# Cross attention with clipped scores: keys on the partitions, one exponential per unit, sums by a product with ones

## The reference, cut to what matters

```
q = state @ Wq            # [128 tokens, 1024], 16 heads of 64
k, v = ctx @ Wkv          # [128 keys, 1024] each
s = (q_h @ k_h.T) * 0.125 # per head, [queries, keys]
s = clip(s, -5, 5)        # and a key that is masked out gets -5
p = exp(s) / sum over keys of exp(s)
out = concat_h(p @ v_h) @ Wo + bo
state = layernorm(state + out)
```

## Time and profile before

| what | value |
|---|---|
| median of 3 runs | 1938.68 us (1937.98 to 1938.98) |
| the profiled execution: its span, first to last instruction | 1932.0 us |
| what lies around the span, median less span | 6.7 us |
| mean granted TensorE clock | 0.960 of full |
| PE, DVE, ACT, POOL busy | 90%, 71%, 69%, 43% |
| L2_xattn in the span | about 970 to 1224 us |

### The profile page before, as it was taken

The page is one execution under the profiler, slowest core; times in us unless marked ns, Lnnn a source line. Parts: engine busy times, 40 slices in busy tenths (PEclk is TensorE's granted clock), DMA queues, the critical chain, the costliest instruction groups (busy, mean ns, idle before and its releaser), DMA issues. The chain is left out here.

```text
span 1932.0 us, 40599 instructions
## 1 busy us (share of the span) xinstructions
PE 1736.0 (90%) x13884; PEld 1294.5 (67%) x13945; DVE 1378.8 (71%) x3901; ACT 1340.0 (69%) x5411; POOL 837.3 (43%) x998
## 2 busy tenths in 40 slices
PE   6999999999888898789999999615889999999998
PEld 6886558889655565246688888404556777777777
DVE  4667886777888898988844444595998656566665
ACT  3447986565899996159977777442988666666666
POOL 2235770000566785147733333121776433333345
PEclk9999999999988999789999999866999999999999
DMA  7000000000000000000000000200000000000000
GB/s 285 1 1 1 2 2 2 1 2 2 2 1 2 2 2 2 1 1 2 2 2 1 2 1 2 117 0 1 1 2 2 1 1 1 1 1 1 1 1 23
DMA packets 5819, 22.98 MB, mean 12 GB/s; under 512 B 624, under 2 KB 2672, under 8 KB 4720
## 3 DMA queue, kind: packets, MB, share of 16 engines
q1 hardware_dynamic: 5616, 20.39, 2.7%
HBM read 19.34 MB, written 1.05 MB: 11 GB/s over the span
## 5 line engine op out<-in xcount | busy, mean ns | idle before, releaser
L1394 POOL TENSOR_TENSOR a_probs<-a_probs,a_rinv 128x512 f32<-128x512 f32 x352 | 365.7, 1040 | 318.0 <-DVE a_rinv L1238 314.5
L1047 ACT ACTIVATE a_probs<-bank,a_negmax 128x128 f32<-128x128 f32 x896 | 324.8, 434 | 12.9 <-DVE a_negmax L1218 12.8
L1394 POOL TENSOR_TENSOR c_probs<-c_probs,c_rinv 128x512 f32<-128x512 f32 x192 | 200.1, 1042 | 163.5 <-DVE c_rinv L1238 160.4
L889 PEld LDWEIGHTS bank<-const,a_probs 128*128 128x128 f32 x1408 | 159.0, 144 | 134.0 <-issue 110.2
L1047 ACT ACTIVATION_READ_ACCUMULATOR a_probs<-bank,a_negmax 128x1 f32 x896 | 237.5, 275 | 0.0
L889 PE MATMUL bank<-const,a_probs 128*128 128x128 f32 x1408 | 231.4, 288 | 1.9 <-DVE a_probs_t L1245 0.9
L1422 POOL TENSOR_TENSOR a_rstd<-a_ve,neg_half 128x1 f32<-128x1 f32 x128 | 70.2, 549 | 341.1 <-DVE a_ve L1296 340.9
L1218 DVE TENSOR_REDUCE a_negmax<-bank 128x4 f32<-128x512 f32 x224 | 152.0, 680 | 20.5 <-PE bank L857 16.6
L857 PE MATMUL bank<-a_kz,a_qk 32*128 32x512 f32 x512 | 148.1, 655 | 2.2 <-DVE a_probs L1216 1.6
L1238 DVE RECIPROCAL a_rinv<-a_rsum 128x4 f32<-128x4 f32 x352 | 59.7, 170 | 113.7 <-ACT a_probs L1043 107.8
L1245 DVE COPY a_probs_t<-bank 128x512 f32<-128x512 f32 x176 | 120.5, 684 | 25.8 <-PE bank L889 24.7
(11 more groups left out here) (254 smaller groups left out, 4418.9 us busy)
## 6 DMA issues: line engine op xcount, KB each, us to landing
w_L_ffn<-in_L_ffn SPq DMA_DIRECT2D x1, 3184.0 KB, 20.4
w_L_xattn<-in_L_xattn SPq DMA_DIRECT2D x1, 2112.0 KB, 29.5
w_L_xattn<-in_L_xattn SPq DMA_DIRECT2D x1, 2050.0 KB, 9.9
w_L_attn<-in_L_attn SPq DMA_DIRECT2D x1, 1345.5 KB, 23.1
w_L_attn<-in_L_attn SPq DMA_DIRECT2D x1, 1157.0 KB, 6.7
ctx_t<-in_ctxT SPq DMA_DIRECT2D x1, 1024.0 KB, 13.0
w_L_attn<-in_L_attn SPq DMA_DIRECT2D x2, 512.0 KB, 14.7
ctx<-in_ctx SPq DMA_DIRECT2D x1, 1024.0 KB, 13.3
```

What stands on the lines that cost most here:

```text
L889: mm = pe.transpose(bank[:, j * S:(j + 1) * S], Pb[:, n % PB, j * S:(j + 1) * S], ident)
L1047: op = act.activation(p, bank_of("scores", n)[:, j * width:(j + 1) * width], ACT.Exp, bias=negmax[:, n % PB, j:j + 1], accum_out=rsum[:, n ...
L1394: pool.tensor_tensor(p, p, along(rinv[:, n % PB, 0:heads], 512 // heads), ALU.mult).then_inc(sems["norm_done"], 1)
```

## The change

The scores are formed with the keys on the output's partitions. The queries lie packed in `Qs` (scaled by 0.125 in one copy), both operands of a head take 64 rows of the array, and the products of the two halves alternate, into two banks; a pair of units is scored together. The clip's upper bound is then one number per partition. One exponential covers the whole unit, without sums. For a pair of units PE forms the sums over the keys by a product with a tile of ones, 64 columns wide, so that the sum stands on all 64 partitions of a head, and then the values, without a transpose before. DVE inverts the bank of sums, 128x512, and multiplies the bank of values by it on the way to `OT` (`divide`, emitted after `inverse` and ahead of the projections' copies in each slot). POOL no longer scales the probabilities. The slots of the stages, of the projections and of the output move. The zeroing block of the first loop is gone. The mask is loaded as 128x16 bytes, element by element.

```diff
-    "h64c": [("q0", 9, "act"), ("q1", 7, "act"), ("k0", 6, "dve"), ("k1", 5, "dve"), ("v0", 4, "act"), ("v1", 2, "act")],
+    "h64c": [("q0", 7, "act"), ("k0", 6, "dve"), ("q1", 5, "act"), ("k1", 4, "dve"), ("v0", 3, "act"), ("v1", 2, "act")],
...
+    "scores": {"all": 3, "h8": 6, "h8p": 6, "h8r": 6, "moe": 4, "h64c": 4, "h64m": 6, "ffn": 4},
+    "max": {"all": 3, "h8": 6, "h8p": 5, "h8r": 6, "h64c": 4, "h64m": 5, "ffn": 4},
+    "front": {"all": 3, "h8": 5, "h8p": 4, "h8r": 5, "lin": 2, "h64c": 3, "h64m": 4},
...
+    "second": {"all": 0, "h64c": 1},
...
+    "values": {"all": -1, "h8": -2, "h8p": -2, "h8r": -2, "h64c": 1},
+    "outs": {"all": -1, "h8": -2, "h8p": -2, "h8r": -2, "h64c": 1, "lin": -2, "ffn": -2},
...
+    "output": {"all": 3, "mqa": 2, "h64c": 1},
+    "stats": {"all": 3, "mqa": 2, "h64c": 1, "lin": 4, "h64m": 4},
+    "normalise": {"all": 5, "mqa": 3, "h8": 4, "moe": 6, "h64c": 3, "h64m": 6, "ffn": 6},
...
-                        pool.memset(Qz[0:64, :, :, 1, :], 0.0)
-                        pool.memset(Qz[64:128, :, :, 0, :], 0.0)
...
+                if was == "values" and kind == "h64c":
+                    wait_once(nc.tensor, sems["divided"], plan.count("divided", m))
+                elif was == "second" and kind == "h64c":
+                    wait_once(nc.tensor, sems["sums_taken"], plan.count("divided", m))
...
+                        if kind == "h64c":
+                            after_reader(pe, s, f"q{i // 2}")
+                            after_reader(pe, s, f"k{i // 2}")
+                            bank_free("scores", n + 1)
+                            for j in range(4):
+                                c = 2 * i + j
+                                for odd in range(2):
+                                    rows = slice(64 * odd, 64 * odd + 64)
+                                    mm = pe.matmul(bank_of("scores", n + odd)[:, j * S:(j + 1) * S], K64[rows, plan.ring(s, 2), c, :], Qs[rows, plan.ring(s, 2), c, :],
+                                                   start=True, stop=True)
...
+                        if kind == "h64c":
+                            if plan.closes(n):
+                                pe.wait_ge(sems["exp_done"], plan.count("exp", n))
+                                bank_free("second", n)
+                                for j in range(4):
+                                    for odd in range(2):
+                                        mm = pe.matmul(bank_of("second", n)[64 * odd:64 * odd + 64, j * S:(j + 1) * S], ones[:, :], Pb[:, (n - 1 + odd) % PB, j * S:(j + 1) * S],
+                                                       start=True, stop=True)
+                                mm.then_inc(sems["second_ready"], 1)
+                                after_reader(pe, s, f"v{i // 2}")
+                                bank_free("values", n)
+                                for j in range(4):
+                                    for odd in range(2):
+                                        h = 4 * (i - 1) + 2 * j + odd
+                                        mm = pe.matmul(bank_of("values", n)[64 * odd:64 * odd + 64, j * S:(j + 1) * S], V64[:, plan.ring(s, 2), 0, h * 64:(h + 1) * 64],
+                                                       Pb[:, (n - 1 + odd) % PB, j * S:(j + 1) * S], start=True, stop=True)
+                                mm.then_inc(sems["values_ready"], 1)
...
-                            for j in range(2):
-                                op = act.activation(Qz[64 * j:64 * j + 64, plan.ring(s, 2), 4 * half:4 * half + 4, j, :],
-                                                    heads_view(bank[64 * j:64 * j + 64, :], 4), ACT.Copy, scale=0.125)
+                            op = act.activation(Qs[:, plan.ring(s, 2), 4 * half:4 * half + 4, :], heads_view(bank[:, :], 4), ACT.Copy, scale=0.125)
...
+                                act.activation(Pb[:, n % PB, :], Pb[:, n % PB, :], ACT.Exp).then_inc(sems["exp_done"], 1)
...
-                            dve.scalar_tensor_tensor(heads_view(Pb[:, n % PB, :], 4), heads_view(bank[:, :], 4), -5.0, over(clip_hi[:, b % MASK_RING, :], 4),
-                                                     ALU.max, ALU.min).then_inc(sems["moved"], 1)
+                            dve.tensor_scalar(Pb[:, n % PB, :], bank[:, :], -5.0, clip_hi[:, b:b + 1], ALU.max, ALU.min).then_inc(sems["moved"], 1)
...
+                    def divide(n):
+
+                        s, i, kind, b = plan.unit(n)
+                        if kind == "h64c" and plan.closes(n):
+                            k = plan.count("divided", n)
+                            dve.wait_ge(sems["second_ready"], plan.count("second", n))
+                            dve.reciprocal(inv[:, k % 2, :], bank_of("second", n)[:, :]).then_inc(sems["sums_taken"], 1)
+                            dve.wait_ge(sems["sums_taken"], k)
+                            dve.wait_ge(sems["values_ready"], plan.count("values", n))
+                            dve.tensor_tensor(OT[:, plan.ring(s, 2), 2 * i - 2:2 * i + 2, :], heads_view(bank_of("values", n)[:, :], 4), heads_view(inv[:, k % 2, :], 4), ALU.mult).then_inc(sems["divided"], 1)
...
+            if name == "mask_bk1":
+                sp.dma_start(to[:, :], of.rearrange("a (g k) -> k (a g)", k=S), allow_slow_non_contiguous=True).then_inc(given_in[name], 16)
+                return
```

More of the change, by code:

```diff
@@ L166, in __init__ @@
             claims += [("scores", m) for m in self.due["scores"].get(n, [])]
-            claims += [("values", m) for m in self.due["values"].get(n, []) if self.kind(self.units[m][0]) not in H8 or self.units[m][1] == 3]
-            claims += [("second", m) for m in self.due["second"].get(n, [])]
+            claims += [("values", m) for m in self.due["values"].get(n, []) if self.closes(m)]
+            claims += [("second", m) for m in self.due["second"].get(n, []) if self.kind(self.units[m][0]) != "h64c" or self.closes(m)]
             for s, name, eng in self.early.get(n, []):
@@ L200, in placed @@
             now = max(m - LEAD[stage].get(kind, LEAD[stage]["all"]), at, before + 1)
-            if stage == "scores" and kind in H8:
+            if stage == "scores" and kind in H8 + ("h64c",):
                 now = at if i % 2 else max(now, at + 1)
@@ L207, in placed, with closes @@
         return slots
+    def closes(self, m):
+        s, i = self.units[m]
+        return i == 3 if self.kind(s) in H8 else i % 2 == 1 if self.kind(s) == "h64c" else True
     def later(self, what, s):
@@ L251, in count @@
             return sum(self.copier(k) == stage for k in range(n + 1))
-        if stage == "values":
-            return sum(self.kind(s) in SOFTMAX and (self.kind(s) not in H8 or i == 3) for s, i in self.units[:n + 1])
+        if stage == "divided":
+            return sum(self.kind(self.units[m][0]) == "h64c" and self.closes(m) for m in range(n + 1))
+        if stage in ("values", "outs"):
+            kinds = SOFTMAX if stage == "values" else TURNED
+            return sum(self.kind(self.units[m][0]) in kinds and self.closes(m) for m in range(n + 1))
+        if stage == "second":
+            return sum(self.kind(self.units[m][0]) in STAGES[stage] and (self.kind(self.units[m][0]) != "h64c" or self.closes(m)) for m in range(n + 1))
         return sum(self.kind(s) in STAGES[stage] for s, _ in self.units[:n + 1])
@@ L734, in probs_free @@
                 for m in before:
-                    wait_once(eng, sems["second_ready"], plan.count("second", m))
+                    if plan.unit(m)[2] == "h64c":
+                        m += not plan.closes(m)
+                        wait_once(eng, sems["values_ready"], plan.count("values", m))
+                    else:
+                        wait_once(eng, sems["second_ready"], plan.count("second", m))
             def hidden_free(eng, n):
@@ L826, in scores @@
                         s, i, kind, b = plan.unit(n)
-                        if kind in H8 and i % 2:
+                        if kind in H8 + ("h64c",) and i % 2:
                             return
@@ L1078, in outs @@
                         s, i, kind, b = plan.unit(n)
-                        if kind in H8 and i < 3:
+                        if kind == "h64c" or not plan.closes(n):
                             return
@@ L1346, in _ @@
                             inverse(m)
+                        for m in plan.due["outs"].get(n, []):
+                            divide(m)
                         for s, name, eng in plan.early.get(n, []):
```

82 lines of the change are left out of this document (38 added, 44 removed), and 3 rows, old and new, of the table LEAD.

## The result

The changed kernel takes 1969.3 us (median of 4 runs, 1968.14 to 1972.83) where the kernel before takes 1938.33 (4 runs on the same chip, 1937.93 to 1938.98). The ratio is 1.0165, interval [1.0151, 1.018]: 31.0 us slower. The forecast was 1959 us, in a range of 1914 to 1992. Direction and mechanism were right; the stage lost 9.4 us more than the sum said. One of the five executions of a later kernel, the one with the copy of K on ACT, took 2809 us at a granted clock of 0.55 and is in no ratio here.

What follows compares the result with a forecast made beforehand. The rewritten stage, bound by PE alone before, was taken to be bound by PE and DVE waiting for each other, 16.8 us a step. Stage +29.2, head -4.8, start -4.0 gave +20.4 us: 1959 us, range 1914 to 1992.

Steps and rivals of the forecast that it cites:

- The reciprocal: DVE's new 128x512 reciprocal out of PSUM, twice a step, taken at 3.35 us each from rows of 4 and 36 elements.
- rival (d): The reciprocal makes eight passes an element and takes 4.4 us: 1991 us in all; chance 0.06.
- Rival (c): The reciprocal costs as any other pass, 0.69 us, leaving the stage PE-bound: 1901 us in all; chance 0.09.
- PE's work: PE's products in the rewritten stage L2_xattn: 13.3 us a step, 2.0 less than before.
- The coupling: PE and DVE wait for each other through shared banks 6 and 7: 10.1 us plus twice the reciprocal, 16.8 a step.
- Rival (b): Looser coupling: PE can run ahead of the K copies, DVE's 13.4 plus some 0.5 us is the period: 1916 us; chance 0.12.
- The sum: First to last output addition 245.4 us against 216.2 (+29.2), head -4.8, start -4.0: +20.4 us in all.
- rival (e): PE's pauses in each step lower the clock to 0.71, PE's part of the chain grows by 2.8 us: 2001 us; chance 0.04.
- Head and start: Before the stage's first addition -4.8 us; at the kernel's start -4.0 us as two memsets between barriers go.
- The mask: The mask's transfer at the start, now 2048 one-byte elements: issue taken near 3 us, adding 0, with +25 us as high end.
- Rival (a): The mask's element transfer holds the kernel's start, 25 us more: 1984 us; chance 0.22.
- The span: Profiled span 1932.0 us against the runs' median 1938.68: 6.7 us taken to lie around the span and stay.

Runs made afterwards that it cites:

- run as the copy: The changed kernel with the 128x512 reciprocal replaced by a copy, so the output is multiplied by the sums: 1907.68 us, ratio 0.9843.

## Why the prediction was right, and where it was short

**The reciprocal.** 3.357 us by the row below (by line and shape: count, busy us, mean ns, idle before), against the 3.35 taken, from a slope between a row of 4 and one of 36 elements. With 1758 ns for 256 columns the slope is (3357 - 1758)/256 = 6.25 ns an element. The four lengths measured (4, 36, 256 and 512 columns) lie within 20 ns of one line with that slope. So the extrapolation over a factor of 14 held. Some luck was in the number: the slope of the two rows, 6.5, gives 3.47 us; the 6.2 that makes 3.35 stands in no row. With 3.47 the walk would have given 17.0, and hidden the error described under the coupling.

```profile
L1279 DVE RECIPROCAL a_inv<-bank 128x512 f32<-128x512 f32 x32 | 107.4, 3357 | 6.6 <-PE bank L946 6.6
```

The eight passes read out of the Trainium skill (VectorE: DVE Perf Modes, "First, the fixed hardware budget") would have been 4.4 us; the measurement decides against that reading, and rival (d) falls. Rival (c), a cheap reciprocal, was run as the copy: 1907.7 us where its working gave 1901.

**PE's work.** The scores of a pair take 1.09 to 1.10 us (1.10 taken), sums and values 0.92 + 0.97 = 1.89 (2.0 taken). But the groups beside them are longer too, and there the count has nothing: where PE never waits (K on ACT, output later) q takes 1.03 to 1.04 ahead of the scores for 0.90, K and V behind the values 1.00 and 0.97 for 0.90 and 0.86. So the period there is 13.54 and not 13.3. The reading of L1526, 64 rows at half clock, was right: the two row halves run beside each other, if the instructions alternate.

**The coupling.** The places of the two waits, PE idle ahead of q0 and of the output behind the K copy, are as forecast, and so is the dependence on R. Rival (b), that PE runs ahead of the copies, is refuted by the waits: it needs DVE as the bound, and DVE is busy for 78%. The period is 17.00 and not 16.8. The walk priced q0 at 0.90 and the output at 1.79, as they run in the kernel before. Here q0 takes 1.09 and the output 1.98, read as distances to the next group in the step above: twice 0.19. (Reciprocal, product and copy took 4.68 instead of 4.74, twice, which gives 0.12 back.) The pause ahead of them is not the reason. In the kernel with the sums copied PE never pauses, and ahead of the scores both take as long, 1.98 and 1.09:

```profile
1106.32 2.04 PE L999 MATMUL bank<-w_L_xattn,a_ot 128*128 128x128 f32 x16
1108.30 1.16 PE L858 MATMUL bank<-a_qs,a_ends 64*128 64x128 f32 x16
...
1113.23 1.16 PE L822 MATMUL bank<-state_t,w_L_xattn 128*128 128x128 f32 x8
1114.32 1.16 PE L858 MATMUL bank<-a_qs,a_ends 64*128 64x128 f32 x16
```

In the kernel with K on ACT and the output one unit later, where v follows the output, it takes 1.79 again:

```profile
1113.02 1.95 PE L999 MATMUL bank<-w_L_xattn,a_ot 128*128 128x128 f32 x16
1114.81 1.02 PE L826 MATMUL bank<-w_L_xattn,ctx_t 128*128 128x512 f32 x2
```

So the 0.19 of the output goes with the 64-row scores that follow. I read it as the switch into the split array, which the prediction named but put wholly into the pair's 1.10; no run isolates it. For q the figure is less firm: ahead of the scores it takes from 0.98 (output one unit later alone) to 1.09.

**The sum.** The mis-sized term is "together 245.4: +29.2"; it measured 254.8, +38.6. The 9.4 us are:
- twelve even periods at +0.2: 2.4.
- the first period, 20.37 instead of 16.8: 3.6. Against an even period of 17.00 it has 3.37 more: the two scores of the step take 2.01 and 1.79 instead of 1.09, q between them 1.84 instead of 1.09, all three in stretches where the granted clock is 0.50 to 0.57, and a v product of 1.00 still stands ahead of that q in the order of the bank uses.
- the last two periods, 16.86 instead of 15.2 and 13.48 instead of 11.8: 3.3. In each the output comes behind a pause for the divide and is 3.45 and 3.64 us long instead of 2.05, which is 3.0 of it.

PE's timeline of the changed kernel, the second scores of the first period with their q, and the last two outputs:

```profile
1010.43 1.21 PE L826 MATMUL bank<-w_L_xattn,ctx_t 128*128 128x512 f32 x2 [2.71 <-DVE a_ends L1203]
1011.43 1.92 PE L822 MATMUL bank<-state_t,w_L_xattn 128*128 128x128 f32 x8
1013.27 1.86 PE L858 MATMUL bank<-a_qs,a_ends 64*128 64x128 f32 x16
...
1240.45 3.45 PE L999 MATMUL bank<-w_L_xattn,a_ot 128*128 128x128 f32 x16 [2.35 <-DVE a_ot L1282]
...
1253.75 3.64 PE L999 MATMUL bank<-w_L_xattn,a_ot 128*128 128x128 f32 x16 [3.30 <-DVE a_ot L1282]
```

So rival (e) was right in kind and wrong in place. The prediction gave the clock a chance only in the even part, where it stayed at 1.00 behind pauses of 1.00 and 1.96 us; it fell at both ends of the stage, where pauses are 2.35 to 3.30 us, and those ends the prediction had walked at the full clock. A granted clock under 1.00 in the stage was one of its own signs of being wrong; the sign came, at the ends.

**Head and start.** The first addition came 2.94 us earlier (1002.72 against 1005.66), from a loop that stood 1.02 us later four steps ahead of it: -4.0 where -4.8 was taken. At the start PE's first product moved from 16.20 to 11.84, -4.4, and the first step's statistics by -5.0 (taken: -4.0). In this pair of profiles 5.7 us of that were lost again in the fourth layer, L1_attn: the statistics start 4.6 us earlier than before's at step 48 and 1.13 later at step 64. Whether this loss goes with the earlier start is open. The profiles speak for it: all ten kernels without the block lose 2.3 to 7.6 us between these steps, at a mean granted clock of 0.82 to 0.89 from 500 to 650 us where before has 0.91, and the one in which the block was put back loses nothing. The medians speak against it: without the block the kernel before gains 2.1 to 5.6 us although its profiled execution lost 7.6 us there. And both profiled executions with the block lie well below the median of their kernel (near 1934 for 1938.7, and 1966.4 for 1974.7), so other executions with the block may have the same loss. Behind the last addition the changed kernel's profile is 1.1 us shorter, which the sum had at nothing. In the medians the parts give -5.0 - 4.0 + 38.6 - 1.1 = 28.5 of the 31.0 us measured, if nothing of the start is lost.

**The mask.** Rival (a) is refuted. SP issued the element transfer at 8.38 us in 2.86 us, where the row transfer took 3.05, and PE starts right behind it:

```profile
8.38 2.86 SPq L1509 DMA_DIRECT2D mask<-in_mask_bk  x1
...
11.84 2.04 PE L795 MATMUL bank<-state_t,w_L_attn 128*128 128x128 f32 x8 [11.84 <-PEq L1521]
```

The transfer did become one packet per element, on the pages' lines on DMA, before's and then after's:

```profile
DMA packets 5819, 22.98 MB, mean 12 GB/s; under 512 B 624, under 2 KB 2672, under 8 KB 4720
```

```profile
DMA packets 7736, 22.71 MB, mean 12 GB/s; under 512 B 2672, under 2 KB 4720, under 8 KB 6640
```

Under 512 B there are 2048 more. The rule of the Trainium skill (DMA: Bandwidth & Descriptors, "Rules for kernel authors") says one descriptor per element for a strided last dimension, and the trace agrees. The price of it appeared nowhere on the path, since the queue's issue didn't grow with the count.

**The span.** The 6.7 us around the span were the wrong name for a right amount: before's profiled execution was faster than its median by the 4.9 us that the 1.8 leave of them.

## What to carry to other kernels

Count not only each engine's work but the loop of hand-overs through shared banks: here PE's work fell by 1.6 to 1.8 us a step (15.35 to 13.54 or 13.79, the periods where it never waits) and DVE stayed under 80% busy, and yet the step grew by 1.65 us, because one 3.36 us instruction stood twice ahead of a copy that freed a bank. When such a long instruction enters an in-order queue, move what others wait for to another engine (27.8 us faster than before, together with a later output), and before you move it ahead in the same queue, ask what it waits for itself: that cost 48 us. Walk the first and the last period of a stage separately, since pauses are longest there.

## What the runs showed of the hardware that I had not expected

The first group behind a long pause of PE can run at 1.2 GHz, half of the full clock: the output's 16 instructions took 3.48 us to the next group behind 3.91 us of idle time (granted clock 0.54), against 1.98 behind 1.00. Behind pauses of 1.00 and 1.96 us in an otherwise busy PE the granted clock stayed at 1.00 in the changed kernel, and yet in the kernel with its halves in turn the scores ran at half speed behind the same 1.96 us and one q group. At the end of the changed kernel's stage the output ran at half speed behind 2.35 us, and the sums at full speed (0.89 us, granted clock 1.00) behind 2.68. So the length of the last pause alone doesn't decide.

A full-array group in front of 64-row products whose halves alternate took up to 0.19 us more than in front of others, with or without a pause ahead of it: the output 1.98 against 1.79, q 0.98 to 1.09 against 0.90. Put against the 0.90 us that the scores of a pair would take at 0.056 us an instruction, the split costs 0.19 in the pair and up to as much again before it.
